# Moving the last group's stages, from the embedding to the output, four slots later

## The reference

```python
x = _gn(x_in)                                  # per channel over the image
y = conv(x, conv_w, rhs_dilation=(5, 5)); y = batchnorm(y)
imp = sigmoid(gelu(y)); xs = x * imp
_, idx = top_k(imp.reshape(B, -1), 192); idx = sort(idx)
tokens = take(xs, idx) + make_pos(H * H, C)[idx]
q, k_, v = split(tokens @ w_qkv.T + b_qkv)     # 8 heads of 4
o = softmax(q k_ / 2) v @ w_o.T + b_o
t1 = layernorm(tokens + o); t2 = layernorm(t1 + relu(t1 @ w1.T + b1) @ w2.T + b2)
x.at[idx].set(t2)                              # the other pixels stay
out = x_in + x
```

## Time and profile before

| what | value |
|---|---|
| median of 3 runs | 1163.62 us (1162.39 to 1167.2) |
| the profiled execution | 1162.26 us |
| its span in the profile | 1160.4 us |
| granted TensorE clock over the span | 0.913 of full speed |
| busy share PE / DVE / ACT / POOL | 81 / 72 / 68 / 54 % |
| mean DMA rate | 214 GB/s |

### The profile page before, as it was taken

One profiled execution on the slowest core, in us unless ns is written; L12 is line 12 of the kernel. 1 busy time (PEld: TensorE's weight loads), 2 busy tenths in 40 slices (PEclk: granted clock), 3 DMA queues, 4 the chain that ended last, 5 costly groups with the idle time before them and its releaser, 6 DMA issues.

```text
span 1160.4 us, 21628 instructions
## 1 busy us (share of the span) xinstructions
PE 938.3 (81%) x6440; PEld 739.5 (64%) x6440; DVE 832.0 (72%) x2075; ACT 788.0 (68%) x1938; POOL 630.2 (54%) x851
## 2 busy tenths in 40 slices
PE   3887867689868997999899989897887588389676
PEld 2665645367747875877687867785665476277544
DVE  5345669368857987898889987996697687455533
ACT  2444654367747786888788878886689488279564
POOL 5322233731567367736774677458535764771442
PEclk9988989799989999999999999999799699799755
DMA  9997987665665999999889999986565466548679
GB/s 240 297 268 225 271 227 215 174 157 152 166 163 146 242 261 260 243 265 277 249 242 267 274 253 236 267 228 171 134 184 149 116 181 176 122 115 236 186 235 274
DMA packets 176252, 247.82 MB, mean 214 GB/s; under 512 B 65512, under 2 KB 71912, under 8 KB 176136
## 3 DMA queue, kind: packets, MB, share of 16 engines
q1 hardware_dynamic: 167944, 244.03, 75.8%
q0 software_dynamic: 8192, 2.40, 1.5%
HBM read 124.53 MB, written 121.80 MB: 212 GB/s over the span
## 4 chain that ended last, share of the span: by engine, by line
PE 37%; DVE 22%; DMA 12%; ACT 10%; POOL 9%; issue 9%; SPq 1%; DVEq 0%; POOLq 0%; ACTq 0%
PE cv L524 11%; PE sc L643 6%; PE xb L508 4%; PE pp L656 4%; PE tr L558 3%; DMA conv_rows<-cvr 3%; ACT wgt L840 3%; DVE res L1347 2%; PE ms L672 2%; DMA table<-xt 2%; PE ib L571 2%; POOL tok_x L1006 2%; DVE junk L1142 2%; POOL tok_imp L1006 2%; ACT pr L869 2%
## 5 line engine op out<-in xcount | busy, mean ns | idle before, releaser
L524 PE MATMUL cv<-X,w_conv 128*128 128x330 f32 (+1 forms) x1024 | 298.2, 418 | 15.1 <-POOL X L980 12.8
L524 PEld LDWEIGHTS cv<-X,w_conv 128*128 128x128 f32 x1024 | 190.2, 201 | 48.1 <-issue 14.6
L840 ACT ACTIVATE wgt<-ib,eps_col,mom 128x440 f32<-128x440 f32 (+1 forms) x256 | 178.7, 705 | 32.7 <-DVE res L1347 19.9
L1142 DVE TENSOR_SCALAR_CACHE_REDUCE junk<-flat,th 128x379 bf16<-128x379 f32 x200 | 120.6, 603 | 93.5 <-ACT th L826 91.9
L1043 POOL TENSOR_SCALAR res<-res,mom 128x440 f32<-128x440 f32 (+1 forms) x152 | 94.7, 626 | 168.5 <-DVE res L1347 166.8
L508 PE MATMUL xb<-cst,X 128*110 128x128 f32 x900 | 150.4, 293 | 43.6 <-ACT xt L806 25.0
L643 PE MATMUL sc<-k_b,qm 128*128 128x192 f32 x768 | 163.8, 339 | 14.0 <-DVE pixf L1242 7.3
L806 ACT COPY xt<-xb 110x512 f32<-110x512 f32 x225 | 131.7, 585 | 50.3 <-PE xb L508 35.9
L1347 DVE SCALAR_TENSOR_TENSOR res<-tr,mom,wgt 128x440 f32<-128x440 f32 (+1 forms) x192 | 121.8, 640 | 43.2 <-PE tr L558 34.4
L869 ACT ACTIVATE pr<-sc,least 128x192 f32<-128x192 f32 x384 | 137.4, 418 | 15.6 <-DVE least L1311 15.3
L1123 DVE BATCH_NORM_STATS2 stats<-X 128x6 f32<-128x458 f32 (+3 forms) x256 | 139.4, 574 | 6.5 <-DMA X<-in_x 6.5
(11 more groups left out here) (169 smaller groups left out, 1544.2 us busy)
## 6 DMA issues: line engine op xcount, KB each, us to landing
table<-xt SPq DMA_DIRECT2D x240, 224.0 KB
rt<-table SPq DMA_DIRECT2D x240, 224.0 KB
out<-res SPq DMA_DIRECT2D x320, 137.5 KB
X<-in_x SPq DMA_DIRECT2D x64, 412.5 KB, 6.2
X<-in_x SPq DMA_DIRECT2D x64, 343.8 KB, 6.6
conv_rows<-cvr SPq DMA_DIRECT2D x64, 188.0 KB
y<-conv_rows SPq DMA_DIRECT2D x64, 165.4 KB
out<-res SPq DMA_DIRECT2D x64, 68.8 KB
```

Source lines behind the costliest of these rows:

```text
L524: last = mm(cv[:, 0:CUT[half]], w_conv[:, 4 * q + z], X[:, m % XI, at0:at0 + CUT[half]], start=z == 0, stop=z == 3)
L840: last = A(wgt[:, n % 2, at0:at0 + w], ib[:, at0:at0 + w], ACT.Identity, scale=mom[:, NB * g + b, 2:3], bias=eps_col[:, 1:2])
L1142: v.tensor_scalar(junk[:, 0:FL], flat[:], th[:, 0:1], None, ALU.is_ge, ALU.add, accum_out=cnt[:]).then_inc(cnt_ok, 1)
```

## The change

A function `place` gives the slot of a step of a group. It is the old one, except that for the last group every step numbered 82 (`EMBED`) or more lies `LATE = 4` slots later. `at` and the end of `SLOTS` go by it.

```diff
-        SLOTS = range(INTO, U * G + BACK + 2)
+        LATE = 4
+
+        def place(g, step):
+
+            return U * g + step + (LATE if g == G - 1 and step >= EMBED else 0)
+
+        taken = {}
+
+        def at(slot, first, n=1):
+
+            if (first, n) not in taken:
+                slots = taken[first, n] = {}
+                for g in range(G):
+                    for k in range(n):
+                        slots.setdefault(place(g, first + k), []).append((g, k))
+            return taken[first, n].get(slot, [])
+
+        SLOTS = range(INTO, place(G - 1, BACK) + U + 2)
...
-        def at(slot, first, n=1):
-
-            g, k = (slot - first) // U, (slot - first) % U
-            return [(g, k)] if k < n and 0 <= g < G else []
```

## The result

The changed kernel took 1168.05 us (median of 20 runs, 1162.99 to 1173.62), the kernel before 1162.51 us (20 runs beside them, 1159.1 to 1167.2): a ratio of 1.0041 [1.0026, 1.0056], or 4.8 us more (the two medians as they stand are 5.5 us apart). That is inside the 0.5 % that counts as no change, but the interval excludes 1: the kernel is slightly slower.

The account below looks back on a forecast made before the run. No engine bounds throughout; group 7's chain sets the time from 1080.11 to 1110.18. Terms +4.4 - 2 + 2.5 - 0.5 = +4.4 us take 1162.26 to 1166.7, or 1168.0 on the median; predicted 1167.6, range 1161.5 to 1172.5.

Parts of the forecast that it names:

- The hole is filled, with little: In PE's 12.8 us idle during the last gathers, group 6's first norm and three slots' units run; embedding doesn't move.
- The projection behind the feed: Group 7's projection now waits for group 6's feed and second first-norm (`v2_ok`), starting at 1017.9, 7.7 us later.
- What that buys: Six score slots without group 6's feed take 13.2 us, so the unit after them could run 2.4 us later.
- the queue passed over: POOL's `masked` precedes group 6's `norm_last`, so unit 0 waits for its load: 4.4 us later in all, bounds 2.4 to 6.
- The scores: Other units, with fewer ACT finishes, stand beside group 7's score slots: 2 us given back, bounds 0 and 4.
- The end: At group 7's scatter, POOL finishes and four SP stores precede its loads: 2.5 us more, bounds 0.6 and 4.
- The tail: During group 7's last units, group 6's last stores are out of the way: 0.5 us less, bounds 0 to 1.5.
- The rule on the clock: After PE's wait, feed and projection run at the low clock; if it stayed up, some 2.6 us less.
- Units are what the end is short of: Rival: units, not group 7's chain, set the time from 1080 on; result 1154 to 1158 us; chance 0.11.
- Near zero: Rival: clock stays up or scores give back 4 us, and stores slip in unseen: +0.5, 1164.1 us; chance 0.17.
- Clearly slower: Rival: group 6's feed takes 9.9 us, scores regain nothing, loads 4 us later: +10, 1173 us; chance 0.2.

Follow-up runs that it names:

- e9: The changed kernel run and profiled once more, no edit: 1164.25 us, ratio 1.0039 to the kernel before.
- e6: The changed kernel's text with LATE = 0, so the instructions and order of the kernel before: 1161.13 us, ratio 1.0010.
- e3: The changed kernel with group 7's V projected into the convolution's PSUM bank, so `project` no longer waits for `v2_ok`: 1159.65 us, ratio 0.9986.
- e10: The changed kernel with group 5's units 14 to 18 finished on ACT instead of POOL: 1164.53 us, ratio 1.0024.
- e5: The changed kernel with group 7's first seven loads at slots 337 and 338, behind `imp_b`, and group 6's units 28 and 29 finished on ACT: 1162.99 us, 1.0020.
- e2: The kernel before with only group 7's steps from the scatter on four slots later: 1163.77 us, ratio 1.0021.
- e8: e4 with group 7's three splits on POOL and `parts_out` fourteen slots later: 1157.42 us, ratio 0.9978.
- e7: The kernel before (LATE = 0) with group 7's V projected into the convolution's PSUM bank: 1155.44 us, ratio 0.9960.
- e11: e8 with group 5's units 14 to 18 finished on ACT: 1156.27 us, ratio 0.9973.
- e4: The changed kernel with LATE = 2, a separate tile for `diag`, and group 7's `value_rows` one slot earlier: 1163.27 us, ratio 1.0010.
- e1: The changed kernel with group 7's first seven loads at slots 335 and 336, and group 6's units 28 and 29 finished on ACT: 1172.7 us, 1.0094.

## Why the prediction was right, step by step

The forecast was 1167.6 us, and the kernel took 1168.05; the sum was +4.4, the ratio says +4.8. That the absolute times agree to 0.5 us is in part luck. The base was a median of 3 runs, 1163.62, and over 20 runs it was 1162.51; and beside e9 the same kernel took 1164.25. Nor does the profile of before bear out the +4.4 that was worked out from it: against it the end moved by 161.34 - 159.08 = 2.3 us, and only against e6, which lacks the dip of the clock, by 4.95. What the prediction got right is the steps. In us after E (the prediction's own times less 1001.32):

| step | predicted | measured (after) |
|---|---|---|
| group 6's feed | 7.4 | 7.78 |
| `v2_ok` | 16.4 | 16.43 |
| projection | 16.6 | 16.58 |
| first scores | 21.1 | 21.13 |
| second `norm_last` of group 6 | 22.7 | 22.63 |
| group 6's unit 0 | 36.3 | 35.10 |
| group 7's mix | 81.2 | 81.01 |
| loads after T | 5.8 | 5.55 |
| first unit of group 7 | 113.8 | 112.96 |
| end | 163.5 | 161.34 |

*The hole is filled, with little: right.* The norm moved by more than 14 us and the feed by 10 (17.80 to 7.78), and the projection didn't follow; it came 7.7 us later.

*The projection behind the feed: right, and shown.* e3 takes the wait for `v2_ok` away: the projection comes 3.8 us earlier, `mix` 4.6, the end 3.8. e10 shortens what the feed waits for: feed and projection come 3.1 us earlier, the end 3.3.

*What that buys, and the queue passed over: 1.2 us too much against the profile used, 0.5 too little against e6, and split wrongly.* I put the unit at +2.4, and +4.4 with its load. Against the profile of before it was +3.2: 2.6 unheld and 0.65 for the load, which I had made 2.0. `norm_last` to the loads took 9.45 us (1031.99 to 1041.44) for 10.6. Against e6, which doesn't have the dip, the term is +4.9. So two mis-sizings met in it: the load overpriced by 1.3, the base too late by 1.7. The six score slots without the feed took 13.97 us, or 13.3 without the wait of 0.65 for the load, where I had 13.2.

*The scores: right in kind, half in size.* -1.0 where I gave -2. The bounds of 0 and 4 held. Which part of it comes from ACT's finishes no run separated.

*The end: right.* +2.0 from `mix` to the first unit against e6, for 2.5. e5 undoes it and gets 2.4 back, in the profile.

*The tail: -0.9 for -0.5,* against e6. Against the profile of before it is -1.8. The old order alone scatters by 1.3 us there (49.30 to 50.57), so the size of this term is known only as 0.6 to 2.3. e5 keeps the shorter tail with the stores later, and e2 gets it without the shift of the front, so it goes with the later scatter and units; what in them shortens it stays open.

*The rule on the clock: agrees.* The granted clock was 1.00 while PE had units, 0.77 in the next stretch and 0.50 in the one where PE waited 10.54 us; the feed took 0.58 us and the projection 0.98, the low-level figures. That is what the Trainium skill (TensorE: Matmul & The Clock Gate, section on HAM oscillation) lets expect. e3 shows the other side: without the 3.43 us of waiting in front, the same projection took 0.54. The 2.6 us that a higher clock would have saved from feed to projection no run separated.

*The rivals.* "Units are what the end is short of" fell: 8.61 us of idle PE stand before the first unit, and e2, with more slots there, is slower than e6. Its condition, that the projection doesn't wait, is met in e8, and there a gain of 4.6 us appears, but from the earlier scores: from `mix` to the first unit it takes 29.67 us, as in e6. "Near zero" would have needed 4 us from the scores. "Clearly slower" needed 9.9 us from feed to `v2_ok`; it was 8.65.

The experiments point to versions that beat both kernels: e7 (0.9960 [0.9938, 0.9981]) and e11 (0.9973 [0.9954, 0.9992]); e8's interval (0.9978 [0.9956, 1.0000]) just reaches 1. By the profile after E, e8 is the shortest, 2.3 us under e7; by the medians e7 is. The intervals overlap, so which is better is open.

## What to carry to other kernels

When a step is moved later to let others fill a hole, list what comes to stand in front of it on every engine: here the projection got behind a feed that waits on POOL's queue, and the loads behind four stores. Price the work that a wait releases as well as the wait: in e4 the projection came 3.9 us earlier than in e6 and the scores 0.3 us later, until POOL's splits were out of the way. List the transfers that a moved load passes, too: in e1 it passed the one that its own first unit needed. And compare two profiles from a common event right ahead of the edit, not from the start of the span, and take more than one profile of the base: the single one used here held 1.7 us that the next didn't have.

## What the runs showed of the hardware

The part ahead of the edit, which is the same in all fourteen profiles in what it issues (e10 and e11 but for five finishes), put E anywhere from 995.9 to 1009.4 us, 13.5 us apart; group 0's last gather already ended between 225.2 and 231.6. Behind E the same instructions repeat within 0.25 us (after and e9), but for dips of the clock with PE busy. The profile of before has one (0.57 granted with PE busy for all of 4 us, where e6 had 1.00), worth 1.7 us; it follows an idle spell of 2.17 us, and e6 has one of 2.15 in the same place and no dip. e4 has one behind 2.31 us of idle PE (eight score matmuls in 2.80 us), and e8, which differs by the place of the splits and `parts_out`, has none behind the same 2.31 us (1.57 us). So behind an idle spell of 2.2 to 2.3 us the clock fell in some executions and not in others. What decides it no run shows, and what scatters the front wasn't tried. With a front that scatters by more than the change is worth, a change of 5 us shows in the ratio only with many runs.
